# GpSimd in a linear-attention layer: additions moved into the matmul loop, and one multiply cut into tiles

## The reference

```python
def _L0_attn_a_ref(x, Wq, Wm, W1, W2, g1, b1, g2, b2):   # x: the normalised input
    q = (x @ Wq).reshape(B, L, H, d)
    feat = jax.nn.elu(q) + 1.0
    KV = jnp.einsum('nshd,nshv->nhdv', feat, q / L)
    Z = 1.0 / (jnp.einsum('nlhd,nhd->nlh', feat, feat.sum(axis=1)) + ATTN_EPS)
    msg = jnp.einsum('nlhd,nhdv,nlh->nlhv', feat, KV, Z) * L
    msg = msg.reshape(B, L, D) @ Wm
    x = x + _layernorm(msg, g1, b1)
    mlp = jax.nn.relu(msg @ W1) @ W2
    x = x + _layernorm(mlp, g2, b2)
    return x
# outside: x = x + _L0_attn_a_ref(_layernorm(x), ...)
```

## Time and profile before

| | us |
|---|---|
| median of 3 runs | 1361.63 |
| the 3 runs | 1357.60, 1361.63, 1362.56 |
| the profiled execution, its time | 1353.68 |
| the profiled execution, its span | 1351.7 |
| first norm, in the span | 0 to 25.4 |
| `linear_attention` | 25.4 to 109.0 |
| `add_normalised` | 109.0 to 180.6 |

### The profile page before, as it was taken

The page is one execution under the profiler, slowest core; times in us unless marked ns, Lnnn a source line. Parts: engine busy times, 40 slices in busy tenths (PEclk is TensorE's granted clock), DMA queues, the critical chain, the costliest instruction groups (busy, mean ns, idle before and its releaser), DMA issues. The chain is left out here.

```text
span 1351.7 us, 31301 instructions
## 1 busy us (share of the span) xinstructions
PE 1049.4 (78%) x9281; PEld 883.3 (65%) x9281; DVE 955.4 (71%) x2968; ACT 682.5 (50%) x1705; POOL 548.8 (41%) x418
## 2 busy tenths in 40 slices
PE   4991331789362899999999999999999998711886
PEld 3991230688242688888788888888888886601886
DVE  6886932566571788887888888888888887530664
ACT  2444410344281566666666666666666664100443
POOL 0006317355000555554455455554545552035554
PEclk9996555899685999999999999999999999555999
DMA  5910043222259565757475665747566540052221
GB/s 142 222 41 0 1 176 129 70 79 75 68 200 266 124 154 149 166 131 171 125 172 142 148 164 138 177 121 174 141 149 159 139 109 1 0 188 94 75 78 52
DMA packets 75273, 165.91 MB, mean 123 GB/s; under 512 B 8249, under 2 KB 54784, under 8 KB 66528
## 3 DMA queue, kind: packets, MB, share of 16 engines
q1 hardware_dynamic: 69600, 152.75, 44.3%
q0 software_dynamic: 5632, 12.67, 2.7%
HBM read 130.76 MB, written 35.67 MB: 123 GB/s over the span
## 5 line engine op out<-in xcount | busy, mean ns | idle before, releaser
L1147 POOL TENSOR_SCALAR ds_scores<-ds_scores,ds_max 128x256 f32<-128x256 f32 x256 | 344.2, 1345 | 332.3 <-DVE ds_max L1366 332.2
L1358 DVE TENSOR_TENSOR ds_p2c<-ds_bank,ds_p2c 128x512 f32<-128x512 f32 x256 | 175.3, 685 | 79.7 <-PE ds_bank L1196 79.3
L1366 DVE CUSTOM_DVE_ANT_0 ds_scores<-ds_bank,ds_p2c 128x256 f32<-128x256 f32 x512 | 195.9, 419 | 0.2 <-DVE ds_p2c L1358 0.2
L1307 ACT ACTIVATE all_xt<-ds_bank 128x512 f32<-128x512 f32 x256 | 154.3, 603 | 77.6 <-PE ds_bank L1214 73.8
L1196 PE MATMUL ds_bank<-all_constants,ds_c2p_t 128*128 128x128 f32 x1024 | 159.5, 278 | 0.0
L1214 PE MATMUL ds_bank<-all_constants,ds_scores 128*128 128x128 f32 x1024 | 154.2, 272 | 1.8 <-ACT all_xt L1307 1.6
L1196 PEld LDWEIGHTS ds_bank<-all_constants,ds_c2p_t 128*128 128x128 f32 x1024 | 116.6, 141 | 35.9 <-issue 24.5
L1214 PEld LDWEIGHTS ds_bank<-all_constants,ds_scores 128*128 128x128 f32 x1024 | 119.6, 140 | 6.8 <-issue 2.2
L1187 PE MATMUL ds_bank<-ds_qr,ds_tab 64*128 64x128 f32 x1024 | 77.1, 292 | 32.5 <-DVE ds_qr L1342 28.9
L1289 ACT ACTIVATE ds_c2p_t<-ds_bank 128x256 f32<-128x256 f32 x256 | 77.8, 400 | 46.5 <-PE ds_bank L1187 46.5
L1203 PE MATMUL ds_bank<-ds_ks,ds_qs 72*128 72x256 bf16 x512 | 98.5, 273 | 2.5 <-DVE ds_max L1366 2.5
(11 more groups left out here) (253 smaller groups left out, 2138.7 us busy)
## 6 DMA issues: line engine op xcount, KB each, us to landing
ds_qr<-scratch_qk SPq DMA_DIRECT2D x32, 1024.0 KB, 10.8
ds_kr<-scratch_qk SPq DMA_DIRECT2D x32, 1024.0 KB, 13.8
ds_tab<-scratch_tables SPq DMA_DIRECT2D x64, 248.0 KB, 9.6
slots_in<-all_zero SPq DMA_DIRECT2D x2, 5160.0 KB, 39.1
ds_qs<-scratch_q_parts SPq DMA_DIRECT2D x32, 288.0 KB
ds_ks<-scratch_k_parts SPq DMA_DIRECT2D x32, 288.0 KB
0fe_xb<-slots_in SPq DMA_DIRECT2D x40, 129.0 KB
1fe_xb<-slots_in SPq DMA_DIRECT2D x40, 129.0 KB
```

The lines of the kernel that those rows point to most:

```text
L1147: pool.tensor_scalar(S[b % NS][:, 1, :], S[b % NS][:, 1, :], mx[:, 2 * b + 1:2 * b + 2], None, ALU.subtract).then_inc(s_sub1, 1)
L1307: act.activation(PT[b], pt2[:, :].rearrange("p (k s) -> p k s", k=2), ACT.Exp).then_inc(s_exp, 1)
L1358: dve.tensor_tensor(z, pt1[b % 2][:, :].rearrange("p (a k) -> p a k", a=2), z, ALU.add).then_inc(s_z, 1)
L1366: last = dve.tensor_tensor_reduce(out=S[b % NS][:, st, :], in0=pqk[b % 2][:, st * SEQ:(st + 1) * SEQ], in1=PC[half][:, st, b, :], scale=1. ...
```

## The change

All additions to `X` that don't depend on the attention leave `add_normalised`. GpSimd makes them in `linear_attention`, a tile at a time: 32 additions of `XN`, the sum of the biases, and 32 additions of that sum. In `add_normalised` GpSimd keeps only the multiply of `ML` by `g2`, now 32 instructions of one tile each, each of which waits for ScalarE to have finished that tile and not its group. VectorE waits for the same things as before, counted anew: for all of GpSimd's additions, and for the eight multiplies of its group.

```diff
@@ linear_attention_layer
-        linear_attention(nc, prefix + "l", con, w, norm.XT, M2, ML, stats, clear_slots)
-        add_normalised(nc, prefix + "a", X, norm, M2, ML, w, stats, switch)
+        both = m.sb("both", [P, D])
+        s_in = m.sem("input")
+
+        def residual(pool):
+
+            for t in range(TILES):
+                pool.tensor_tensor(X[:, t, :], X[:, t, :], norm.XN[:, t, :], ALU.add).then_inc(s_in, 1)
+            pool.wait_ge(w.s_gb, 64)
+            pool.tensor_tensor(both[:, :], w.bias[:, 0, :], w.bias[:, 1, :], ALU.add).then_inc(s_in, 1)
+            pool.wait_ge(s_in, TILES + 1)
+            for t in range(TILES):
+                pool.tensor_tensor(X[:, t, :], X[:, t, :], both[:, :], ALU.add).then_inc(s_in, 1)
+
+        linear_attention(nc, prefix + "l", con, w, norm.XT, M2, ML, stats, clear_slots, residual)
+        add_normalised(nc, prefix + "a", X, norm, M2, ML, w, stats, switch, s_in)
@@ linear_attention
             clear_slots(sp)
+
+        @block.gpsimd
+        def _(pool):
+            residual(pool)
@@ add_normalised, GpSimd
             pool.wait_ge(w.s_gb, 64)
-            pool.tensor_tensor(both[:, :], bias[:, 0, :], bias[:, 1, :], ALU.add).then_inc(s_both, 1)
-            pool.wait_ge(s_both, 1)
-
-            def residual(g):
-                x = X[:, GT * g:GT * (g + 1), :]
-                pool.tensor_tensor(x, x, norm.XN[:, GT * g:GT * (g + 1), :], ALU.add).then_inc(s_in, 1)
-                pool.wait_ge(s_in, 2 * g + 1)
-                pool.tensor_tensor(x, x, both[:, :].unsqueeze(1).to_broadcast([P, GT, D]), ALU.add).then_inc(s_in, 1)
-
-            residual(0)
-            for g in range(TILES // GT):
-                if g + 1 < TILES // GT:
-                    residual(g + 1)
-                pool.wait_ge(s_norm, 2 * GT * (g + 1))
-                part = ML[:, GT * g:GT * (g + 1), :]
-                pool.tensor_tensor(part, part, gain[:, 1, :].unsqueeze(1).to_broadcast([P, GT, D]), ALU.mult).then_inc(s_gain, 1)
+            for t in range(TILES):
+                pool.wait_ge(s_norm, 2 * (t + 1))
+                pool.tensor_tensor(ML[:, t, :], ML[:, t, :], gain[:, 1, :], ALU.mult).then_inc(s_gain, 1)
@@ add_normalised, VectorE
                     if what is not None:
-                        dve.wait_ge(s_in, 2 * g + 2)
+                        dve.wait_ge(s_in, 2 * TILES + 1)
@@
-                dve.wait_ge(s_gain, g + 1)
+                dve.wait_ge(s_gain, GT * (g + 1))
                 dve.tensor_tensor(x, x, b, ALU.add).then_inc(s_x, 1)
```

More of the change, by code:

```diff
@@ L497, in linear_attention_layer, with linear_attention @@
         stats = m.sb("stats", [P, 2, TILES, 6])
-        linear_attention(nc, prefix + "l", con, w, norm.XT, M2, ML, stats, clear_slots)
-        add_normalised(nc, prefix + "a", X, norm, M2, ML, w, stats, switch)
-def linear_attention(nc, prefix, con, w, XT, M2, ML, stats, clear_slots):
+        both = m.sb("both", [P, D])
[10 more added lines that the diff above has]
+        add_normalised(nc, prefix + "a", X, norm, M2, ML, w, stats, switch, s_in)
+def linear_attention(nc, prefix, con, w, XT, M2, ML, stats, clear_slots, residual):
     with ExitStack() as stack:
@@ L672, in _, with add_normalised @@
             over_steps(dve, step)
-def add_normalised(nc, prefix, X, norm, M2, ML, w, stats, switch):
+def add_normalised(nc, prefix, X, norm, M2, ML, w, stats, switch, s_in):
     with ExitStack() as stack:
         m = Mem(nc, stack, prefix)
-        gain, bias = w.gain, w.bias
-        both = m.sb("both", [P, D])
+        gain = w.gain
         diff = m.sb("diff", [P, 2 * TILES])
@@ L685, in add_normalised @@
         shift = m.sb("shift", [P, 2 * TILES])
-        s_diff, s_sq, s_var, s_sum, s_ve, s_std, s_rstd, s_neg, s_shift, s_norm, s_gain, s_both, s_in, s_x = (m.sem(n) for n in (
-            "diff", "square", "var", "sum", "vareps", "std", "rstd", "neg", "shift", "norm", "gain", "both", "input", "x"))
+        s_diff, s_sq, s_var, s_sum, s_ve, s_std, s_rstd, s_neg, s_shift, s_norm, s_gain, s_x = (m.sem(n) for n in (
+            "diff", "square", "var", "sum", "vareps", "std", "rstd", "neg", "shift", "norm", "gain", "x"))
         GT = norm.GT
```

## The result

The changed kernel took 1341.69 us (median of 4 runs, 1338.53 to 1344.39), the kernel before 1359.62 in the same comparison (4 runs, 1356.81 to 1362.56). The ratio is 0.9871, with a 95% interval of 0.9844 to 0.9899: 1.3% faster. The forecast was 1346.4, between 1341 and 1355. The profiled execution took 1341.81 us, its span 1339.8.

The account below looks back on a forecast made before the run. The prediction took VectorE, held up by GpSimd, to bound `add_normalised` except at its start, where it waits for ScalarE. Gains of 15.7 us less 0.5 in the loop gave 15.2 less: 1346.4 us, range 1341 to 1355.

Parts of the forecast that it names:

- table load to first L702: Start of `add_normalised`: VectorE's small instructions no longer wait for GpSimd's additions; L702 begins near 111.8, not 117.2; gain 5.4 us.
- group 0, three instructions: VectorE's L760, L760 and L764 in `add_normalised`: 9.83 us become 4.77, one-tile multiplies coming between; gain 5.1 us.
- its L115: VectorE's L115 after each group's three in `add_normalised` meets no GpSimd instruction: gain 2.1 us in group 0, 0.9 in group 1.
- group 1, three: VectorE's three instructions of group 1 in `add_normalised`: 5.62 us become 4.44; gain 1.2 us.
- group 2, three, and L123 behind: `add_normalised`: one multiply now comes between the three, the last two fall in the eight L123, 4.16 us before; gain 1.0.
- p: Cost of a one-tile GpSimd instruction to a VectorE instruction it excludes: taken as 0.33 us, bounds 0.29 and 0.59.
- The loop: `linear_attention`: VectorE's waits for GpSimd's additions cost 0.5 us, 0.3 at the first copy and 0.25 in the steps.
- the sign given for the loop's block: Profile after: `linear_attention` takes 83.6 to 84.5 us, with GpSimd done in it by 47 to 64 us.
- (1): Rival: a small GpSimd instruction is dear, 0.59 us; gain only 7.4 us, time 1354.2; chance 0.10.
- (3): Rival: ScalarE becomes the bound from group 1 of `add_normalised` on; gain 12.1 us, time 1349.5; chance 0.08.
- (4): Rival: the change does nothing, what `add_normalised` gains is waited for after it; time 1361.6 us; chance 0.04.
- (2): Rival: GpSimd's unbroken run of 32 loop instructions keeps VectorE's L671 and one L655 waiting; 13.7 us slower, 1375.3; chance 0.06.

## Why the prediction was right

Step by step for `add_normalised`, the times from the start of one instruction to the start of the next:

| step | before | forecast gain | after | gain |
|---|---|---|---|---|
| table load to first L702 | 7.92 | 5.4 | 2.43 | 5.5 |
| group 0, three instructions | 9.83 | 5.1 | 4.34 | 5.5 |
| its L115 | 2.20 | 2.1 | 0.08 | 2.1 |
| group 1, three | 5.62 | 1.2 | 4.15 | 1.5 |
| its L115 | 1.00 | 0.9 | 0.08 | 0.9 |
| group 2, three, and L123 behind | 3.77 + 4.08 | 1.0 | 3.90 + 2.40 | 1.5 |
| small losses at L115 and the first L123 | | | | -0.2 |
| sum | | 15.7 | | 16.8 |

The mechanism held at every step, and so did the rule that only some instructions of VectorE are touched: in the loop only the copies and the small multiply ever grew. The one term that was off is p, the wait that a one-tile multiply leaves behind between two of VectorE's. I took 0.33 us for all; 0.30 is right for the first, where GpSimd starts just ahead, 0.13 for most of the others, 0.23 for one in group 1 (1.46 for 1.23, GpSimd 0.07 us ahead) and 0.17 each for the two in the L123 of group 2. That makes the 1.1 us by which the block gained more than forecast. As a duration 0.33 was too low, since GpSimd's instruction lasts 0.46, and the 65 in the loop took 26.6 us and not 21.5; but duration and exclusion are not the same thing, which the pairs of tiles showed, and nobody waited for the end of GpSimd's list.

The loop was forecast at 0.5 us, between 0.3 and 5.6: 0.3 for the first copy and 0.25 for the steps. At like pace it is 0.2 to 0.3, and all of it is the first copy (L688, 0.55 us for L671's 0.29). In the steps L672 was held in the first few, up to 0.62 us, and L675 in one step of two of the three profiles (0.47 and 0.45), and the slack of the step swallowed it: that term is nothing. What the forecast didn't know is TensorE's slow stretch at the start of the loop, whose end moves by itself. So the sign given for the loop's block, 83.6 to 84.5 us, failed in the first profile (86.90) although GpSimd did as forecast. The profiled execution was to take 1338.5 us and took 1341.8: 1.1 us better in the block, 2.7 worse in the loop, 0.9 and 0.8 worse ahead of it and behind.

Of the rivals, (1) fell with 0.13 for 0.59. (3) came near: ScalarE's idle time before L148 shrank from 8.3 to 0.7 us, as forecast (1.1), but did not vanish. (4) fell: what follows L225 took 1171.8 and 1171.0 us in the first pair. (2) did not happen in the changed kernel in three profiles, but the 8.2 us with 96 more additions is what it describes, once. The rows of L719 and L760 show the normal case, in which GpSimd stands back, but don't exclude the other.

The measured 1341.69 us is inside the range, but only 0.7 us above its lower end, which was the sum with no multiply in the way at all and 2.3 us of scatter. The medians differ by 17.9 us where 15.2 were forecast. The block's p explains 1.1 of that and the loop 0.3; the other 1.3 us have no place in the mechanism.

What stays open: the profiles give 16.8 - 0.2 = 16.6 us for the change, a ratio of 0.9878. The two timed comparisons, 0.9871 and 0.9847, are 17.5 and 20.8 us, and the interval of the second ends at 0.9872. The kernels with one part of the change were timed in that second comparison too, and gained 16.5 and 6.0 us where their blocks and the loop give 11.8 and 2.6. All three thus gained 3.4 to 4.7 us more than the profiles show; they are set against the same executions of the kernel before, so this is one deviation and not three, and its cause isn't shown. The rest after L225 ranges from 1169.8 to 1179.6 us over all kernels with no order by kernel, and the change of pace moves the loop by 3 us, so single profiles can't resolve it. No profile shows a place for a further gain of the change.

## What to carry to other kernels

In this kernel work on GpSimd "beside" VectorE was not free where VectorE's instructions have two SBUF inputs or are copies or tensor_scalar instructions from SBUF to SBUF: it was paid for on VectorE (16.8 us in one block), and appeared there as busy time, so look for instructions that take far more than their like. Such work belongs in a stage where VectorE mostly reads PSUM and has some idle time in each step, and in pieces no longer than that idle time. If it must stay, cut it so finely that each piece starts as soon as its data is there, which puts most of it into VectorE's idle time.

## What the runs showed of the hardware that was not expected

- A GpSimd instruction of one tile lasts 0.46 us and holds VectorE up for 0.30 when it begins just ahead, for 0.13 when it has itself waited for VectorE. Two tiles then cost 0.40, an eight-tile multiply 2.0.
- VectorE's small multiply in the loop, whose scalar operand lies in PSUM and the rest in SBUF, is held up like one from SBUF to SBUF: 2.12 us for 0.23.
- Between GpSimd instructions that follow each other without a wait, VectorE is normally let in after the current one. Once in two profiles with 161 such instructions a copy waited for some 20 of them, 8.2 us.
- In the first steps of the first matmul loop TensorE's matmuls take nearly twice their later time, 1.19 for 0.61 us. In five of the 14 profiles the granted clock is recorded as 0.50 for just that time, in nine as 1.00 all through or nearly so: a recorded 1.00 does not prove full speed here, the matmuls' own durations do. In four of the five the first four matmuls ran fast (0.68) and the clock fell behind them. The faster pace has come by 33 us, or only one step later, by 39 to 44, with the same kernel at either, and the loop takes up to 3 us more for it.
